# Attention: the weighted values of a row tile's eight heads in one run of 128 products instead of two runs of 64, with twelve slots of transposed exponentials

## The chip, the cores and the metric

The kernel runs on one core of a Trainium2 chip. The metric is the device time of one execution in microseconds (us), lower is better. Before the change it is 2987.2 us, the median of 3 runs (2986.61 to 2988.67).

## The reference, cut to what matters

Eight graphs (the batch) of 1024 nodes with 256 features pass through four layers, each behind a layer norm with ReLU and with a residual. The change touches the second, an attention with eight heads of 32 features, whose scores are multiplied by the adjacency matrix before the softmax:

```python
q, k, v = (proj(Wq, bq), proj(Wk, bk), proj(Wv, bv))      # 8 heads of 32
scores = jnp.einsum('bhqd,bhkd->bhqk', q, k) * SCALE
scores = scores * (adj_matrix + bond_matrix)[:, None]     # both are adj
attn = jax.nn.softmax(scores, axis=-1)
ctx = jnp.einsum('bhqk,bhkd->bhqd', attn, v)
return jnp.einsum('bse,fe->bsf', ctx.reshape(...), Wo) + bo
```

All data is float32; the matrix of adjacencies is 1024 x 1024 for each graph.

## The kernel before

The program runs the batch elements one after the other, all four layers of one before the next. The order of the work on each engine is written out by hand; engines meet through counting semaphores (`signal`), of which the name tells what is ready (`exps`: exponentials, `T_ps`: transposes in PSUM, `pv_ps`: weighted values in PSUM).

The attention part of an element is a pipeline over 64 **units**. Unit u is one head of one row tile: 128 query rows (tile t = u // 8) against all 1024 keys. For each unit:

- TensorE makes the scores, 128 x 1024, in two products (L1288), into one of two pairs of PSUM banks.
- VectorE multiplies them by the adjacency rows and takes the row maximum in one pass, `Z`, 128 x 1024 (L790). GpSimd negates the maximum (L566, `nm`).
- ScalarE takes the exponential in place with its row sum (L1046). `Z` has three slots (`ZS`).
- TensorE transposes `Z` in eight 128 x 128 blocks (L1310) into two of three PSUM banks in turn, four blocks to a bank.
- ScalarE copies the first bank out (L1036) and VectorE the second (L745) to a **slot** of transposed exponentials, `PT(u)`, 128 x 8 x 128. For the unit with u % 8 = 5, ScalarE copies both. The eight slots lie in three tiles: `PTa` four, `PTz` one, `PTb` three.
- TensorE multiplies `v` by the slots (L1339, weighted values): a product has 32 output rows, one head, and four heads stand side by side in the array. A group of four heads needs 32 products in the program, which are 64 TensorE instructions in the trace (two each). Each row tile has two groups (`GROUPS`), in two parts of PSUM bank 7.

Once both groups of a row tile are done, VectorE multiplies them by the spread inverse sums (`normalise`, L758, `ctxn`), TensorE multiplies by the output weights (`project`, L1122 on `Wo,ctxn`) and VectorE adds the result to `x` (L765).

Every engine walks the same steps u = 0, 1, ... On TensorE step u is: `project` if one is due, `scores(u + 2)`, weighted values of a group if one is due, `transposes(u)`, and the spread of the inverse sums if due. A group g is due at step 4g + 7: the first group of row tile t at step 8t + 7, the second at 8t + 11. On VectorE step u is: `Z(u)`, then `normalise`, `add_output` and statistics where they are due, then the copy of unit u - 2. On ScalarE it is the exponential of u, then the copy of unit u - 1. GpSimd also builds the 0/1 matrix `H` for the next layer in the steps' gaps (L578).

Behind the last row tile TensorE starts the third layer with `first_edges` (L1369, L1370), then the last `project` and `sum_up` (L1403). The matrix `adjT`, on whose place `PTa`, `Z` and `PTz` lie in the attention part, is loaded again in three parts by SyncE as its tenants are done (L486). At the start of the part the stacked operands `qS` and `kS` are put together by DMAs out of `khi`, `klo`, `qhi` and `qlo` (L411); `PTb` lies behind these four.

Of the kernel before, what the change touches and what calls it, by code (L numbers as in the profile page):

```python
# [5 lines left out]
F32 = mybir.dt.float32  # L6
# [25 lines left out]
def build_program(nc, x_in, adj_in, adjT_in, mask_in, wqkT0, wv0, w1attn, bq1, bk1, bv1, bo1,  # L32
# [13 lines left out]
    BOTH = 5  # L46
    PTS = 8
    PTA = 4
# [15 lines left out]
    with ctx:  # L64
# [3 lines left out]
        def signal(name, per):  # L68
            return Signal(ctx.enter_context(nc.semaphore(name)), per)
# [50 lines left out]
        def _bytes(shape):  # L120
            n = 4
            for s in shape[1:]:
# [34 lines left out]
             ("W1", [P, 3, DT, D], F32)],  # L157
            [("stacked", [P, 4, GROUPS, N], F32), ("PTb", [P, PTS - PTA - 1, NT, P], F32), ("rs", [P, HEADS, HD], F32), ("Rs", [P, GROUPS, P], F32)],
            [("h2", [P, NT, HID], F32), ("h2T", [P, FT, N], F32)],
# [6 lines left out]
        khi, klo, qhi, qlo, hT1, W1 = p1a  # L166
        _, PTb, rs, Rs = p1b
        h2, h2T = p2
# [81 lines left out]
        PT_dve = signal("PT_dve", UNITS - NT)  # L250
        pv_ps = signal("pv_ps", NT * GROUPS)
        R_ps = signal("R_ps", NT)
# [61 lines left out]
        INVERT, SPREAD, COPY, WEIGH, NORMALISE, PROJECT, ADD = 4, 4, 7, 7, 9, 10, 11  # L314
        PARTS = (NT,)

# [24 lines left out]
        def turn_bank(use):  # L341
            return 4 + turns.index(use) % TBANKS
# [56 lines left out]
        def PT(u):  # L399

            slot = u % PTS
            return PTa[:, slot] if slot < PTA else PTz if slot == PTA else PTb[:, slot - PTA - 1]

        def heads_of(t):
            return t[:, :].rearrange("p (a n) -> p a n", n=P)
# [11 lines left out]
        def _(sp):  # L417
# [38 lines left out]
            def batch(b, last):  # L456
# [30 lines left out]

                sp.wait_ge(*pv_ps(b, NT * GROUPS - 1))
                stand(sp, waited_sp)
# [130 lines left out]
        def _(dve):  # L620
# [49 lines left out]
            def batch(b, last):  # L670
# [67 lines left out]
                def evacuate(u):  # L738
                    if evacuates_both(u):
                        return  # L740
                    bank = turn_bank((u, 1))
                    dve.wait_ge(*T_ps(b, 2 * u + 2))
                    if u >= PTS:
                        dve.wait_ge(*pv_ps(b, (u - PTS) // HPG + 1))
                    dve.tensor_copy(PT(u)[:, NT // 2:NT], heads_of(ps[:, bank])).then_inc(PT_dve.sem, 1)  # L745

                def inverse_sums(t):
# [4 lines left out]
                def normalise(t):  # L752
                    dve.wait_ge(*pv_ps(b, GROUPS * (t + 1)))
                    if t == NT - 1:
                        dve.wait_ge(*Rss(b, t + 1))
                    if t:
                        dve.wait_ge(*o_ps(b, t))
                    dve.tensor_tensor(ctxn[:], ps[:, 7, 0:GROUPS * P].rearrange("p (g n) -> p g n", n=P), Rs[:],  # L758
                                      ALU.mult).then_inc(ctxs.sem, 1)
# [206 lines left out]
        def _(act):  # L966
# [8 lines left out]
            def batch(b, last):  # L975
# [52 lines left out]

                def evacuate(u):
                    for half_of_u in range(1 + evacuates_both(u)):  # L1030
                        bank = turn_bank((u, half_of_u))
                        act.wait_ge(*T_ps(b, 2 * u + half_of_u + 1))
                        if u >= PTS:
                            act.wait_ge(*pv_ps(b, (u - PTS) // HPG + 1))
                        first = NT // 2 * half_of_u
                        act.activation(PT(u)[:, first:first + NT // 2], heads_of(ps[:, bank]), ACT.Copy).then_inc(PT_act.sem, 1)  # L1036
# [81 lines left out]
        def _(pe):  # L1118
# [46 lines left out]
            def batch(b, first):  # L1165
# [155 lines left out]

                def weighted_values(g, part):


                    if part == 0:
                        pe.wait_ge(*PT_act(b, by_act(HPG * g + HPG - 1)))
                        t = g // GROUPS
                        if g == 0:
                            pe.wait_ge(*vs(b, NT // 2))
                        if g % GROUPS and t < NT - 1:  # L1330
                            pe.wait_ge(*Rss(b, t + 1))
                        if g % GROUPS == 0 and t:
                            pe.wait_ge(*ctxs(b, t))
                    for kt in range(sum(PARTS[:part]), sum(PARTS[:part + 1])):
                        if kt == NT // 2:
                            pe.wait_ge(*PT_dve(b, by_dve(HPG * g + HPG - 1)))
                        for j in range(HPG):
                            hd = ORDER[HPG * (g % GROUPS) + j]
                            mm = pe.matmul(ps[HD * j:HD * j + HD, 7, P * (g % GROUPS):P * (g % GROUPS + 1)],  # L1339
                                           v[:, kt, HD * hd:HD * hd + HD], PT(HPG * g + j)[:, kt],  # L1340
                                           start=(kt == 0), stop=(kt == NT - 1))
                    if part == len(PARTS) - 1:
                        mm.then_inc(pv_ps.sem, 1)

# [27 lines left out]
                for u in range(STEPS):  # L1372
# [6 lines left out]
                    if u + 2 < UNITS:  # L1379
                        scores(u + 2)  # L1380
                    for part in range(len(PARTS)):
                        if (g := group_due(u, WEIGH + part)) is not None:
                            weighted_values(g, part)
                    if u in BESIDE:
# [196 lines left out]
```

## Time and profile before

| | |
|---|---|
| median of 3 runs | 2987.2 us |
| span of the profiled execution, first to last instruction | 2986.1 us |
| TensorE matmul busy | 2935.2 us (98%) |
| TensorE weight load busy | 2371.0 us (79%) |
| VectorE busy | 1879.2 us (63%) |
| ScalarE busy | 1491.5 us (50%) |
| GpSimd busy | 720.8 us (24%) |
| mean granted TensorE clock | 0.999 of full speed |
| chain of work that ended last | TensorE 68%, VectorE 14%, issue 11%, GpSimd 4%, ScalarE 3% |

The profile gives for the profiled execution its span, and no device time of its own beside it; the span lies 1.1 us under the median of the timed runs. The busy shares are means over four layers with different limits, so what the change does has to be read from the attention part of one batch element. In the element used below that part runs from about 455 us to 602 us of the span. Within it a row tile of eight units repeats every 16.6 us.

### The profile page before, as it was taken

The numbers are of one execution on the slowest core, as the hardware profiler recorded it, in microseconds if no ns is written. First come the engines' busy times: TensorE is split into PE (matmuls) and PEld (weight loads), VectorE is DVE, ScalarE is ACT, GpSimd is POOL, SyncE is SP. The second block draws the span as 40 slices with busy tenths as digits, with TensorE's granted clock in tenths as the row PEclk, the third lists the DMA queues.
The fourth block names the chain that finished last, engine by engine and source line by source line (L and its number), as shares of the span: only waits on it lengthen the run. The fifth ranks groups of instructions, "written<-read, shape, count | busy, mean of one in ns | idle before, by whom it ended". The sixth has DMA issues, their size and how long they took to land.

```text
span 2986.1 us, 63496 instructions
## 1 busy us (share of the span) xinstructions
PE 2935.2 (98%) x23040; PEld 2371.0 (79%) x23040; DVE 1879.2 (63%) x4154; ACT 1491.5 (50%) x2761; POOL 720.8 (24%) x1305
## 2 busy tenths in 40 slices
PE   8999999999999999999999999999999999999999
PEld 7888787887878878888788886888868888688886
DVE  3797427874278742887428874388643886438863
ACT  2883317833288232873228732387323873238622
POOL 0343003420134201342013420134201341014410
PEclk9999999999999999999999999999999999999999
DMA  5202212022120231101311113111222022220200
GB/s 175 93 2 93 91 58 93 2 92 111 49 83 13 81 131 38 74 34 60 135 48 61 54 50 124 61 48 59 62 108 78 30 73 69 87 81 27 83 8 14
DMA packets 95317, 204.29 MB, mean 68 GB/s; under 512 B 10512, under 2 KB 41616, under 8 KB 94992
## 3 DMA queue, kind: packets, MB, share of 16 engines
q1 hardware_dynamic: 93456, 195.76, 17.9%
q8 instruction: 203, 3.33, 0.5%
q0 software_dynamic: 1536, 4.20, 0.4%
q14 instruction: 122, 1.00, 0.1%
HBM read 136.75 MB, written 8.65 MB: 49 GB/s over the span
## 4 chain that ended last, share of the span: by engine, by line
PE 68%; DVE 14%; issue 11%; POOL 4%; ACT 3%; DVEq 0%; DMA 0%; POOLq 0%; ACTq 0%; SPq 0%
PE ps L1122 39%; PE ps L1310 8%; PE ps L1403 7%; PE ps L1288 4%; PE ps L1478 4%; PE ps L1339 4%; DVE junk L832 3%; POOL H L578 3%; DVE Z L790 2%; DVE stats L629 1%; DVE h L848 1%; DVE dn L841 1%; DVE h L866 1%; POOL nm L566 1%; PE ps L1162 1%
## 5 line engine op out<-in xcount | busy, mean ns | idle before, releaser
L790 DVE CUSTOM_DVE_ANT_0 Z<-ps,adjN 128x1024 f32<-128x1024 f32 x512 | 624.0, 1219 | 69.3 <-PE ps L1288 67.1
L1046 ACT ACTIVATE Z<-Z,nm 128x1024 f32<-128x1024 f32 x512 | 587.4, 1147 | 54.2 <-POOL nm L566 54.1
L1310 PE MATMUL ps<-ident,Z 128*128 128x128 f32 x4096 | 545.9, 276 | 19.4 <-ACT Z L1046 16.9
L1310 PEld LDWEIGHTS ps<-ident,Z 128*128 128x128 f32 x4096 | 458.6, 140 | 129.4 <-issue 59.7
L1288 PE MATMUL ps<-kS,qS 128*128 128x512 f32 x1024 | 370.2, 444 | 3.3 <-issue 3.3
L578 POOL TENSOR_SCALAR H<-adjN 128x128 fp32r<-128x128 f32 (+1 forms) x456 | 316.6, 694 | 0.0
L566 POOL TENSOR_TENSOR nm<-nm,minus 128x1 f32<-128x1 f32 x512 | 97.1, 190 | 646.9 <-DVE nm L790 642.1
L1122 PE MATMUL ps<-mh,adjT 128*128 128x256 f32 x1024 | 223.6, 379 | 0.8 <-issue 0.8
L1122 PE MATMUL ps<-v,P 128*128 128x257 f32 x1024 | 223.6, 379 | 0.0
L1122 PE MATMUL ps<-hT,t3T 128*128 128x512 f32 x512 | 221.0, 592 | 0.0
L1122 PEld LDWEIGHTS ps<-v,P 128*128 128x128 f32 x1024 | 193.8, 189 | 31.9 <-issue 3.8
L1122 PEld LDWEIGHTS ps<-mh,adjT 128*128 128x128 f32 x1024 | 193.9, 190 | 27.2 <-issue 1.2
L745 DVE COPY PTa<-ps 128x512 f32<-128x512 f32 x256 | 176.0, 687 | 31.8 <-PE ps L1310 31.8
L1122 PEld LDWEIGHTS ps<-hT,t3T 128*128 128x128 f32 x512 | 97.3, 190 | 119.1 <-issue 118.6
L543 POOL TENSOR_SCALAR ve<-mv 128x4 f32<-128x4 f32 x64 | 12.6, 197 | 724.5 <-DVE mv L634 723.9
L686 DVE CUSTOM_DVE_ANT_0 E<-ps,G 128x256 f32<-128x256 f32 x64 | 27.2, 425 | 252.4 <-PE ps L1122 209.4
L1122 PE MATMUL ps<-W,hT 128*128 128x256 f32 x768 | 178.3, 382 | 0.8 <-ACT hT L980 0.8
L1036 ACT ACTIVATE PTb<-ps 128x512 f32<-128x512 f32 x256 | 144.2, 588 | 59.0 <-PE ps L1310 59.0
L1288 PEld LDWEIGHTS ps<-kS,qS 128*128 128x128 f32 x1024 | 159.5, 191 | 13.9 <-issue 8.2
L1036 ACT ACTIVATE PTa<-ps 128x512 f32<-128x512 f32 x256 | 150.8, 589 | 38.9 <-PE ps L1310 38.9
L1106 ACT ACTIVATE E<-ps,cj 128x512 f32<-128x512 f32 x128 | 87.9, 687 | 159.6 <-PE ps L1122 159.6
L1122 PEld LDWEIGHTS ps<-W,hT 128*128 128x128 f32 x768 | 143.5, 192 | 23.9 <-issue 1.0
(183 smaller groups left out, 5713.5 us busy)
## 6 DMA issues: line engine op xcount, KB each, us to landing
adjT<-adjT_in SPq DMA_DIRECT2D x8, 4096.0 KB, 13.0
adjN<-adj_in SPq DMA_DIRECT2D x8, 4096.0 KB, 17.6
adjT<-adjT_in SPq DMA_DIRECT2D x8, 2048.0 KB, 7.7
qS<-qhi SPq DMA_DIRECT2D x112, 128.0 KB, 2.1
qS<-qlo SPq DMA_DIRECT2D x112, 128.0 KB, 2.1
adjT<-adjT_in SPq DMA_DIRECT2D x8, 1536.0 KB, 12.0
xn<-x_in SPq DMA_DIRECT2D x8, 1024.0 KB, 5.7
out<-x SPq DMA_DIRECT2D x8, 1024.0 KB, 4.8
```

The source lines that it names most:

```text
L566: pool.tensor_tensor(nm[:, u:u + 1], nm[:, u:u + 1], minus[:], ALU.mult).then_inc(nms.sem, 1)
L578: done = pool.tensor_scalar(H[:, t, of], adjN[:, t, of], 0.0, 0.0, ALU.is_equal, ALU.is_equal)
L745: dve.tensor_copy(PT(u)[:, NT // 2:NT], heads_of(ps[:, bank])).then_inc(PT_dve.sem, 1)
L790: dve.tensor_tensor_reduce(Z[:, u % ZS], ps[:, 2 * (u % 2):2 * (u % 2) + 2].rearrange("p a n -> p (a n)"), adjN[:, u // HEADS], SCORE_SCAL ...
L1036: act.activation(PT(u)[:, first:first + NT // 2], heads_of(ps[:, bank]), ACT.Copy).then_inc(PT_act.sem, 1)
L1046: act.activation(Z[:, u % ZS], Z[:, u % ZS], ACT.Exp, bias=nm[:, u:u + 1], accum_out=sm[:, u:u + 1]).then_inc(exps.sem, 1)
L1122: mm = pe.matmul(dst, lhsT, rhs, start=(i == 0), stop=(i == len(pairs) - 1))
L1288: mm = pe.matmul(ps[:, 2 * (u % 2) + s], qS[:, hd, rows(t)], kS[:, hd, half(s)], start=True, stop=True)
L1310: mm = pe.transpose(ps[:, turn_bank((u, s)), rows(a)], Z[:, u % ZS, rows(NT // 2 * s + a)], ident[:])
L1339: mm = pe.matmul(ps[HD * j:HD * j + HD, 7, P * (g % GROUPS):P * (g % GROUPS + 1)], v[:, kt, HD * hd:HD * hd + HD], PT(HPG * g + j)[:, kt], ...
L1403: mm = pe.matmul(dst(n, i), lhs(n, j, i), rhs(n, j, i), start=(j == 0 and i == 0), stop=(j == NT - 1 and i == 0))
L1478: mm = pe.matmul(ps[:, bank(t), 0:D], HT[:, j, rows(t)], (Vh, Vl)[i][:, j], start=(j == 0 and i == 0), stop=(j == NT - 1 and i == 0))
```

## The change

The weighted values of both groups of a row tile are made in one run, `weighted_values(t)`, due where the second group was: step 8t + 11. The run at step 8t + 7 is gone. For that, a row tile's first four slots are held four units longer, and there are twelve slots instead of eight. The four new ones, `PTc`, lie behind `khi` and `klo`, where `qhi` and `qlo` are, so the copies of unit 8, the first into `PTc`, wait for the seven DMAs that read `qhi` and `qlo` (`qS_in`). `pv_ps` counts row tiles instead of groups, and all waits on it are rewritten. The last row tile uses slots 4 to 11 so that `PTa` is free once the last but one is done, and SyncE's first part of the `adjT` reload waits for that.

```diff
     BOTH = 5
-    PTS = 8
+    PTS = 12
     PTA = 4
...
              ("W1", [P, 3, DT, D], F32)],
-            [("stacked", [P, 4, GROUPS, N], F32), ("PTb", [P, PTS - PTA - 1, NT, P], F32), ("rs", [P, HEADS, HD], F32), ("Rs", [P, GROUPS, P], F32)],
+            [("keys", [P, 2 * GROUPS * N + 16], F32), ("PTc", [P, PTA, NT, P], F32), ("PTb", [P, PTS - 2 * PTA - 1, NT, P], F32), ("rs", [P, HEADS, HD], F32), ("Rs", [P, GROUPS, P], F32)],
             [("h2", [P, NT, HID], F32), ("h2T", [P, FT, N], F32)],
...
         PT_dve = signal("PT_dve", UNITS - NT)
-        pv_ps = signal("pv_ps", NT * GROUPS)
+        pv_ps = signal("pv_ps", NT)
         R_ps = signal("R_ps", NT)
...
         INVERT, SPREAD, COPY, WEIGH, NORMALISE, PROJECT, ADD = 4, 4, 7, 7, 9, 10, 11
-        PARTS = (NT,)
...
-            slot = u % PTS
+            slot = u % PTS if u < UNITS - HPG else u % PTS + HPG
+            if slot >= 2 * PTA:
+                return PTc[:, slot - 2 * PTA]
             return PTa[:, slot] if slot < PTA else PTz if slot == PTA else PTb[:, slot - PTA - 1]
...
-                sp.wait_ge(*pv_ps(b, NT * GROUPS - 1))
+                sp.wait_ge(*pv_ps(b, NT - 1))
                 stand(sp, waited_sp)
...
                     bank = turn_bank((u, 1))
+                    stacks_read(u)
                     dve.wait_ge(*T_ps(b, 2 * u + 2))
                     if u >= PTS:
-                        dve.wait_ge(*pv_ps(b, (u - PTS) // HPG + 1))
+                        dve.wait_ge(*pv_ps(b, (u - PTS) // HEADS + 1))
                     dve.tensor_copy(PT(u)[:, NT // 2:NT], heads_of(ps[:, bank])).then_inc(PT_dve.sem, 1)
+
+                def stacks_read(u):
+                    if u == 2 * PTA:
+                        for s in range(NH):
+                            for j in range(len(qS_in[s])):
+                                dve.wait_ge(*qS_in[s][j](b, 64))
...
                 def normalise(t):
-                    dve.wait_ge(*pv_ps(b, GROUPS * (t + 1)))
+                    dve.wait_ge(*pv_ps(b, t + 1))
                     if t == NT - 1:
...
                 def evacuate(u):
+                    if u == 2 * PTA:
+                        for s in range(NH):
+                            for j in range(len(qS_in[s])):
+                                act.wait_ge(*qS_in[s][j](b, 64))
                     for half_of_u in range(1 + evacuates_both(u)):
...
                         if u >= PTS:
-                            act.wait_ge(*pv_ps(b, (u - PTS) // HPG + 1))
+                            act.wait_ge(*pv_ps(b, (u - PTS) // HEADS + 1))
                         first = NT // 2 * half_of_u
...
-                def weighted_values(g, part):
-
-
-                    if part == 0:
-                        pe.wait_ge(*PT_act(b, by_act(HPG * g + HPG - 1)))
-                        t = g // GROUPS
-                        if g == 0:
-                            pe.wait_ge(*vs(b, NT // 2))
-                        if g % GROUPS and t < NT - 1:
-                            pe.wait_ge(*Rss(b, t + 1))
-                        if g % GROUPS == 0 and t:
-                            pe.wait_ge(*ctxs(b, t))
-                    for kt in range(sum(PARTS[:part]), sum(PARTS[:part + 1])):
-                        if kt == NT // 2:
-                            pe.wait_ge(*PT_dve(b, by_dve(HPG * g + HPG - 1)))
-                        for j in range(HPG):
-                            hd = ORDER[HPG * (g % GROUPS) + j]
-                            mm = pe.matmul(ps[HD * j:HD * j + HD, 7, P * (g % GROUPS):P * (g % GROUPS + 1)],
-                                           v[:, kt, HD * hd:HD * hd + HD], PT(HPG * g + j)[:, kt],
-                                           start=(kt == 0), stop=(kt == NT - 1))
-                    if part == len(PARTS) - 1:
-                        mm.then_inc(pv_ps.sem, 1)
+                def weighted_values(t):
+
+                    if t == 0:
+                        pe.wait_ge(*vs(b, NT // 2))
+                    else:
+                        pe.wait_ge(*ctxs(b, t))
+                    if t < NT - 1:
+                        pe.wait_ge(*Rss(b, t + 1))
+                    for g in range(GROUPS):
+                        first = HEADS * t + HPG * g
+                        pe.wait_ge(*PT_act(b, by_act(first + HPG - 1)))
+                        for kt in range(NT):
+                            if kt == NT // 2:
+                                pe.wait_ge(*PT_dve(b, by_dve(first + HPG - 1)))
+                            for j in range(HPG):
+                                hd = ORDER[HPG * g + j]
+                                mm = pe.matmul(ps[HD * j:HD * j + HD, 7, P * g:P * (g + 1)],
+                                               v[:, kt, HD * hd:HD * hd + HD], PT(first + j)[:, kt],
+                                               start=(kt == 0), stop=(kt == NT - 1))
+                    mm.then_inc(pv_ps.sem, 1)
...
                         scores(u + 2)
-                    for part in range(len(PARTS)):
-                        if (g := group_due(u, WEIGH + part)) is not None:
-                            weighted_values(g, part)
+                    if (t := tile_due(u, WEIGH)) is not None:
+                        weighted_values(t)
                     if u in BESIDE:
```

The order of TensorE's instructions shows the move. In the listings the names are those of tiles: `Z` on `ident` are transposes, `kS,qS` are scores, `rs` is the spread of the inverse sums, `PTa`, `PTz`, `PTb` and `PTc` on `v` are weighted values; a listing gives program instructions, of which a float32 product becomes two in the trace where its source does. The first place is TensorE from step 14 to step 17 of the first batch element, at the transposes of unit 14. Before:

```order
L1310 MATMUL ps<-ident,Z 128x128 x8
L1288 MATMUL ps<-kS,qS 128x512 x2
L1339 MATMUL ps<-PTa,v 32x128 x32
L1310 MATMUL ps<-ident,Z 128x128 x8
L1288 MATMUL ps<-kS,qS 128x512 x2
L1310 MATMUL ps<-ident,Z 128x128 x8
L1318 MATMUL ps<-ident,rs 128x128 x2
L1288 MATMUL ps<-kS,qS 128x512 x2
L1310 MATMUL ps<-ident,Z 128x128 x8
```

Now:

```order
L1322 MATMUL ps<-ident,Z 128x128 x8
L1300 MATMUL ps<-kS,qS 128x512 x2
L1322 MATMUL ps<-ident,Z 128x128 x8
L1300 MATMUL ps<-kS,qS 128x512 x2
L1322 MATMUL ps<-ident,Z 128x128 x8
L1330 MATMUL ps<-ident,rs 128x128 x2
L1300 MATMUL ps<-kS,qS 128x512 x2
```

The run of 32 products on `PTa` between the scores of unit 17 and the transposes of unit 15 is gone; nothing else moved.

The second place is TensorE at steps 18 and 19, beginning with the scores of unit 20. Before (the last two rows come seven more times):

```order
L1288 MATMUL ps<-kS,qS 128x512 x2
L1310 MATMUL ps<-ident,Z 128x128 x8
L1288 MATMUL ps<-kS,qS 128x512 x2
L1339 MATMUL ps<-PTz,v 32x128
L1339 MATMUL ps<-PTb,v 32x128 x3
```

Now:

```order
L1300 MATMUL ps<-kS,qS 128x512 x2
L1322 MATMUL ps<-ident,Z 128x128 x8
L1300 MATMUL ps<-kS,qS 128x512 x2
L1350 MATMUL ps<-PTc,v 32x128 x32
L1350 MATMUL ps<-PTa,v 32x128 x32
L1322 MATMUL ps<-ident,Z 128x128 x8
```

Where 32 products on slots 4 to 7 stood, 64 stand now: first those of the row tile's first four heads (`PTc`), then those of the other four (`PTa`), and the transposes of unit 19 come behind both.

## Rows read from the trace of the kernel before

**Rows 1.** The page of the profile: its first line, and one line of DMA issues.
```profile
span 2986.1 us, 63496 instructions
...
qS<-qlo SPq DMA_DIRECT2D x112, 128.0 KB, 2.1
```

**Rows 2.** Windows view, one row tile: start:end, then busy us and (instructions) of each engine.
```profile
503.30:519.90 16.60, 16.36 (x219) 13.68 (x221) 15.02 (x29) 14.19 (x27) 7.20 (x17) 1.00 0.01 2
```

**Rows 3.** Chain of work that ended last, second batch element: start, us, what.
```profile
486.74 1.88 PE ps L1339 x64
...
569.72 1.88 PE ps L1339 x64
```

**Rows 4.** Timeline, all engines, 511 to 529: start, us, engine, instruction, [idle before <-releaser].
```profile
513.67 1.09 PE L1310 MATMUL ps<-ident,Z 128*128 128x128 f32 x8
...
514.80 0.69 DVE L745 COPY PTb<-ps 128x512 f32<-128x512 f32 x1 [0.63 <-PE ps L1310]
...
515.46 1.23 DVE L790 CUSTOM_DVE_ANT_0 Z<-ps,adjN 128x1024 f32<-128x1024 f32 x1
...
516.08 0.71 PE L1288 MATMUL ps<-kS,qS 128*128 128x512 f32 x2
...
516.62 1.04 PE L1310 MATMUL ps<-ident,Z 128*128 128x128 f32 x8
...
517.00 1.15 ACT L1046 ACTIVATE Z<-Z,nm 128x1024 f32<-128x1024 f32 x1 [0.42 <-POOL nm L566]
...
518.37 1.09 PE L1310 MATMUL ps<-ident,Z 128*128 128x128 f32 x8 [0.24 <-ACT Z L1046]
...
519.21 0.72 PE L1288 MATMUL ps<-kS,qS 128*128 128x512 f32 x2
...
519.86 0.31 PE L1339 MATMUL ps<-PTb,v 128*32 128x128 f32 x3
...
521.53 0.28 PE L1339 MATMUL ps<-PTb,v 128*32 128x128 f32 x3
...
521.74 1.09 PE L1310 MATMUL ps<-ident,Z 128*128 128x128 f32 x8
...
521.88 0.42 DVE L758 TENSOR_TENSOR ctxn<-ps,Rs 128x256 f32<-128x256 f32 x1
...
522.87 0.69 DVE L745 COPY PTa<-ps 128x512 f32<-128x512 f32 x1 [0.57 <-PE ps L1310]
...
527.16 1.15 ACT L1046 ACTIVATE Z<-Z,nm 128x1024 f32<-128x1024 f32 x1
527.30 1.22 DVE L790 CUSTOM_DVE_ANT_0 Z<-ps,adjN 128x1024 f32<-128x1024 f32 x1 [0.29 <-PE ps L1288]
```

**Rows 5.** Waits, 486.74 to 586.3 (six row tiles): who waited: us, times, longest.
```profile
DVE PTb L745 <- PE ps L1310: 3.8, 6, 0.6
DVE PTa L745 <- PE ps L1310: 3.4, 6, 0.6
```

**Rows 6.** Timeline, all engines, 476 to 485 (start of the attention part).
```profile
477.85 1.16 ACT L1046 ACTIVATE Z<-Z,nm 128x1024 f32<-128x1024 f32 x1
...
479.60 0.60 SPq L411 DMA_DIRECT2D qS<-qlo  x1
...
481.62 0.69 DVE L745 COPY PTb<-ps 128x512 f32<-128x512 f32 x1 [0.57 <-PE ps L1310]
```

**Rows 7.** Timeline, all engines, 593 to 602 (end of the attention part).
```profile
593.90 1.14 ACT L1046 ACTIVATE Z<-Z,nm 128x1024 f32<-128x1024 f32 x1
...
596.54 1.09 PE L1310 MATMUL ps<-ident,Z 128*128 128x128 f32 x8
...
597.88 0.30 PE L1339 MATMUL ps<-PTz,v 128*32 128x128 f32 x1
...
599.76 0.39 PE L1369 MATMUL ps<-hh,H 128*128 128x258 f32 x1
...
600.96 1.13 PE L1122 MATMUL ps<-Wo,ctxn 128*128 128x256 f32 x4 [0.22 <-DVE ctxn L758]
```

More of the change, by code:

```diff
@@ L166, in build_program @@
         khi, klo, qhi, qlo, hT1, W1 = p1a
-        _, PTb, rs, Rs = p1b
+        _, PTc, PTb, rs, Rs = p1b
         h2, h2T = p2
```

## The prediction

> **What bounds the kernel now.** I read the windows first, then the chain, then the timeline of one row tile, then the waits, then the two ends of the attention part.
>
> The windows view of one row tile [rows 2] shows TensorE busy for 16.36 of 16.60 us, VectorE 15.02, ScalarE 14.19 and GpSimd 7.20, with the granted clock at 1.00. That looks like a kernel bound by TensorE with VectorE 9% behind, but such shares don't tell who waits for whom. The chain of work that ended last gives the pace: second runs of weighted values start at 486.74 and 569.72 with four between, so a row tile takes (569.72 - 486.74) / 5 = 16.60 us [rows 3]. The profile's page gives the span of 2986.1 [rows 1], against which the sum below is made; the median of the timed runs is 1.1 us above it.
>
> The timeline of row tile 2 and 3 [rows 4] shows how the two engines pass the limit between them. Three places matter.
>
> At the second run (step 27): scores start at 519.21, the run at 519.86, and the transposes of unit 27 behind it at 521.74. VectorE does `Z(29)` meanwhile, so it gets through almost the whole run; `ctxn` starts at 521.88, as soon as the run is done. Then it waits 0.57 us for the transposes (copy at 522.87). From here TensorE sets the pace until VectorE's `Z(32)` at 527.30, which waited 0.29 for its scores.
>
> At the first run (the one of the row tile before ends where the transposes of unit 23 start, 513.67): VectorE waits 0.63 us for them (copy at 514.80).
>
> After that VectorE sets the pace: its copy leads to `Z(26)` at 515.46, over GpSimd's negation to the exponential at 517.00 (waited 0.42 for GpSimd), which ends a little before TensorE's transposes of unit 26 at 518.37 (waited 0.24 for ScalarE). So TensorE has a little idle time ahead of the second run, and VectorE none. The waits view over six row tiles [rows 5] has both waits once in each: 3.8 and 3.4 us in 6 times each. This is all that VectorE loses to the two runs: 1.2 us in a row tile, though they hold TensorE for 3.8 us, because a run of 1.9 us is nearly covered by the VectorE work that is queued up when it starts.
>
> **The change, part by part.**
>
> The length of a run. From scores to the next transposes TensorE takes 521.74 - 519.21 = 2.53 us with a run between and 516.62 - 516.08 = 0.54 without [rows 4], so a run costs it 1.99. The last of its sixteen packs of four instructions starts 1.67 after the first of the rows, 519.86 and 521.53, so a pack takes 0.11 and sixteen more take 1.76. The other 0.23 is paid at the run's two ends. The long run therefore costs 1.99 + 1.76 = 3.75, and a row tile's total on TensorE falls by 0.23.
>
> The added part, 64 instructions more at step 8t + 11: +1.76 us. The work that covers the run now, `Z(29)`, ends just when the present run does (`ctxn` starts at 521.88, 0.07 behind the run's end). `Z(30)` stands behind `ctxn` and the copy of unit 27 on VectorE, and both wait for the run; ScalarE's exponential of unit 29 stands behind the copy of unit 27 too. So nothing is left to cover the added 1.76, and all that follows on all three engines moves by it: `ctxn`, transposes of unit 27, `Z(32)` from 527.30 to 529.06. Bounds: 1.76 if nothing covers it; 1.53 if the 0.23 of the saved ends fell here, which I exclude, since those ends are at the other run.
>
> The removed part, the run ahead of the transposes of unit 31 (as of unit 23 in the rows). Those transposes start one row tile after 513.67, at 530.27 now. Without the run they start when the exponential of unit 31 is done. It starts at 527.16 + 1.76 = 528.92, takes 1.24 to its end and the next 0.12 to the transposes (517.00 to 518.37 is 1.37 in all): 530.29. So on TensorE the delay is fully made up at this point, and this is the trap: VectorE isn't made up. It is 1.76 late at `Z(32)`, works without a pause until the copy of unit 31, and there it finds its transposes done, so the 0.63 wait is gone. Behind that copy it is late by 1.76 - 0.63 = **1.13 us**, and from there VectorE sets the pace up to the transposes of unit 34 and the next run. Each row tile is 1.13 longer, 17.73 instead of 16.60. Bounds: had `Z(32)` also won back its 0.29 wait, 0.84; but that wait is for scores that moved with the rest. If only half of the 0.63 comes back, because TensorE or ScalarE is late behind the exponential of unit 31, 1.45. I take 1.13.
>
> There are six such distances from run to run in one element (row tile 0 to 6).
>
> The start. Row tile 0 loses its first run. Copy of unit 7 waited 0.57 there (481.62), the exponential of unit 7 starts at 477.85 and so its transposes could start at 479.2 [rows 6]: **-0.57**. From zero to that.
>
> The end. Behind row tile 6's run the exponential of unit 63 moves by 1.76, from 593.90 to 595.66, and its transposes can start 1.37 later, at 597.03, where they stood at 596.54 [rows 7]. The last run starts 597.88 - 596.54 = 1.34 behind them, at 598.37, and takes 599.76 - 597.88 + 1.76 = 3.64: `first_edges` at 602.01 instead of 599.76. The last `project` stood 1.20 behind `first_edges`, 0.22 of it waiting for `ctxn`, a wait that is gone since `ctxn` needs only the run: 602.01 + 0.98 = 602.99 instead of 600.96, **+2.0**. Up to +2.6 if the spread of the sums ahead of the run is late with the exponential. The next layer starts from there with TensorE without a gap, so I see nothing that gives it back.
>
> The new slots. `PTc` makes both copies of unit 8 wait for the last `qS` DMA. It is issued at 479.60 and lands 2.1 later [rows 6, 1], at 481.7; the first copy of unit 8 comes more than half a microsecond behind the start of the copy of unit 7, now at 481.05, so at about 482. Cost nothing; if the landing took 3 us, 0.6 an element. The wait instructions themselves run while the exponential and `Z` ahead of them do. All other waits on `pv_ps` ask for a run at least one step old, so cost nothing. The earlier reload of `adjT` gives nothing: no engine is in the chain for it.
>
> The sum for one element: -0.57 + 6 x 1.13 + 2.0 = 8.2 us; for eight, 65.7. 2986.1 + 65.7 = 3051.8 as a span, and with the 1.1 of the median above it **3053 us**, 2.2% slower.
>
> **The rivals.**
>
> *TensorE's work alone counts (faster).* TensorE is busy for 16.36 of 16.60 us; if it were the bound throughout, the place of the runs would not matter and each row tile would gain the 0.23 of one run's two ends: 64 x 0.23 = 15, so 2972. This decides once VectorE's and ScalarE's queued work at the run's start is longer than the run, 3.75; it is 521.88 - 519.86 = 2.0 in the rows. Against it speak both waits of rows 5 as well. 6%. The Trainium skill has the rule behind this rival (TensorEngine Tiling (Array Packing), Key Properties): changing the tiling mode of the array drains it. Half the runs are half the changes between 128 x 128 and 128 x 32. The trace agrees that the ends cost something, the 0.23 above; by the rule alone the change would be the gain of 15 us, by the trace it is the smaller term.
>
> *The delay is made up (no change, or little).* TensorE is back on time at unit 31, 530.29 against 530.27. If VectorE could follow, each row tile would cost nothing and the ends remain: 8 x (2.0 - 0.57) = 11, so 2998; with the start's gain alone and the end covered, 2983. VectorE has no slack in between, so 6% for both, of which 3% within 0.2%.
>
> *Half made up, or less than in the forecast.* A row tile costs 0.3 to 0.8: 3010 to 3035. 8%.
>
> *Nothing is won back.* 1.76 a row tile, 2.6 at the end, nothing at the start: 8 x (10.6 + 2.6) = 106, so 3093; with half of the wait won back, 3068 to 3075. 6% beyond the range.
>
> **How the numbers follow.** The forecast, with the bounds of its terms from 1.0 to 1.4 a row tile, has 74% and spans 3040 to 3072. The range is 3030 to 3072; about 2 in 10 is left out. A measurement of this kernel can't tell less than about 0.2% (6 us) from no change. Faster by more than that: 7%. Within it: 4%. Slower: 89%.
>
> **What the changed kernel's profile would show.** Runs of 128 instructions 17.7 us apart, each about 3.6 us long. VectorE's wait ahead of `ctxn` new, 1.6 to 1.8 us each; the 0.57 behind it as now; the 0.63 at the copies of units with u % 8 = 7 gone. VectorE busy for the same time in a longer row tile, and TensorE at 16.1 of 17.7. The exponential of units with u % 8 = 2 still waits for GpSimd. The prediction is wrong if `ctxn` waits under 1 us (then more work covers the run than I see), if a wait for `qS` DMAs stands ahead of the copies of unit 8, or if the row tile takes 16.4.

## The result and the profile after

The changed kernel takes 3039.97 us, the median of 4 runs (3038.86 to 3041.77), against 2987.93 for the kernel before beside it. The ratio is 1.0176, with a 95% interval of 1.0162 to 1.019: 52 us slower, where 3053 (66 us slower) was forecast, in a range of 3030 to 3072. The profiled execution has a span of 3037.1, 51.0 more than before. The page's first lines:

```profile
span 3037.1 us, 63580 instructions
...
PE 2956.9 (97%) x23040; PEld 2362.0 (78%) x23040; DVE 1873.8 (62%) x4154; ACT 1490.7 (49%) x2761; POOL 721.0 (24%) x1305
```

TensorE has the same 23040 instructions and is busy 22 us longer by the page: the busy time of pipelined matmuls is no count of work.

The chain of work that ended last (start, us, what) gives the pace as in [rows 3]: second batch element, the first and the sixth run of weighted values, the last one, and the start of the third layer's sums.

```profile
492.79 3.63 PE ps L1350 x128
...
580.44 3.63 PE ps L1350 x128
...
610.03 3.63 PE ps L1350 x128
...
615.43 11.22 PE ps L1412 x94
```

A row tile takes (580.44 - 492.79) / 5 = 17.53 us instead of 16.60. It is so in all eight batch elements: by the starts of `ctxn` on VectorE, row tile 1 to 5, a row tile takes 17.46 to 17.58, where it took 16.57 to 16.60. The timeline of one row tile (all engines, 526 to 546), in the order of [rows 4]:

```profile
527.13 0.72 PE L1300 MATMUL ps<-kS,qS 128*128 128x512 f32 x2
...
527.77 0.30 PE L1350 MATMUL ps<-PTz,v 128*32 128x128 f32 x1
...
531.40 1.09 PE L1322 MATMUL ps<-ident,Z 128*128 128x128 f32 x8
531.54 0.42 DVE L766 TENSOR_TENSOR ctxn<-ps,Rs 128x256 f32<-128x256 f32 x1 [1.71 <-PE ps L1350]
...
532.53 0.69 DVE L747 COPY PTa<-ps 128x512 f32<-128x512 f32 x1 [0.57 <-PE ps L1322]
...
536.96 1.23 DVE L798 CUSTOM_DVE_ANT_0 Z<-ps,adjN 128x1024 f32<-128x1024 f32 x1 [0.29 <-PE ps L1300]
...
538.12 1.15 PE L1322 MATMUL ps<-ident,Z 128*128 128x128 f32 x8
...
540.25 0.18 DVE L635 BATCH_NORM_AGGREGATE mv<-stats 128x2 f32<-128x6 f32 x1
540.34 0.66 DVE L747 COPY PTb<-ps 128x512 f32<-128x512 f32 x1
...
540.92 1.22 DVE L798 CUSTOM_DVE_ANT_0 Z<-ps,adjN 128x1024 f32<-128x1024 f32 x1
```

The run lies between the scores at 527.13 and the transposes at 531.40: 4.27 us, 3.73 more than the 0.54 without a run. `ctxn` (L766) has a wait of 1.71 ahead of it that was not there before; the wait of 0.57 at the copy behind it, and that of 0.29 at `Z(32)` (536.96), are as they were. The copy of unit 31 (540.34), where 0.63 was waited, starts without a wait. The waits view over six row tiles (492.79 to 598) shows the new wait as the only one of its size on VectorE:

```profile
DVE ctxn L766 <- PE ps L1350: 10.3, 6, 1.7
```

At the start of the attention part (timeline of the changed kernel, 476 to 492) the copy of unit 7 (487.72) no longer waits. The last `qS` DMA is issued at 487.04, lands 2.1 later by the page's median [rows 1], at about 489.14, and the first copy into `PTc`, of unit 8, starts at 489.30. The exponential's last piece, its row sum, starts 0.13 ahead of that copy, where it is 0.09 at the copy of unit 7, so the new DMA waits cost 0.04 at most here. The margin of 0.16 is thin, though.

```profile
483.60 1.22 DVE L798 CUSTOM_DVE_ANT_0 Z<-ps,adjN 128x1024 f32<-128x1024 f32 x1 [1.90 <-PE ps L1300]
...
487.04 0.60 SPq L412 DMA_DIRECT2D qS<-qlo  x1
...
487.72 0.69 DVE L747 COPY PTb<-ps 128x512 f32<-128x512 f32 x1
...
489.30 0.60 ACT L1048 ACTIVATE PTc<-ps 128x512 f32<-128x512 f32 x1
```

To measure the two ends, two lines of the kernel before are needed beside [rows 3]: its `Z(8)` in the timeline, and its start of the third layer's sums in the chain.

```profile
476.85 1.22 DVE L790 CUSTOM_DVE_ANT_0 Z<-ps,adjN 128x1024 f32<-128x1024 f32 x1 [1.89 <-PE ps L1288]
```

```profile
602.09 11.22 PE ps L1403 x94
```

From `Z(8)` to the first full run: 486.74 - 476.85 = 9.89 before, 492.79 - 483.60 = 9.19 after, so -0.70. From there to the third layer's sums: 602.09 - 486.74 = 115.35 before, 615.43 - 492.79 = 122.64 after, +7.29, of which six row tiles take 6 x 0.93 = 5.6 and the end 1.7. Per element 6.6, for eight 53; the spans differ by 51.0.

### The profile page after: what moved, and what is told of

Same layout as the page of the kernel before. It is cut to its first block, busy times and chain, and to the rows that moved or that the text cites. A ratio compares the mean times of both kernels' runs of the same rounds, so it can differ in the third digit from the quotient of the medians.

```text
span 3037.1 us, 63580 instructions
## 1 busy us (share of the span) xinstructions
PE 2956.9 (97%) x23040; PEld 2362.0 (78%) x23040; DVE 1873.8 (62%) x4154; ACT 1490.7 (49%) x2761; POOL 721.0 (24%) x1305
## 4 chain that ended last, share of the span: by engine, by line
PE 67%; DVE 14%; issue 9%; ACT 3%; POOL 3%; SPq 2%; DMA 1%; DVEq 0%; POOLq 0%; ACTq 0%
PE ps L1134 37%; PE ps L1322 7%; PE ps L1350 7%; PE ps L1412 7%; PE ps L1487 4%; PE ps L1300 4%; DVE junk L840 3%; POOL H L579 2%; DVE Z L798 2%; SPq L412 2%; DVE stats L630 1%; ACT Z L1058 1%; DVE h L856 1%; DVE dn L849 1%; DVE h L874 1%
## 5 line engine op out<-in xcount | busy, mean ns | idle before, releaser
L1322 PEld LDWEIGHTS ps<-ident,Z 128*128 128x128 f32 x4096 | 448.6, 140 | 216.3 <-issue 126.9
L1322 PE MATMUL ps<-ident,Z 128*128 128x128 f32 x4096 | 557.2, 279 | 52.4 <-ACT Z L1058 40.9
L927 DVE TENSOR_TENSOR P<-E,adjT 128x512 f32<-128x512 f32 x128 | 88.7, 693 | 113.6 <-ACT E L1118 113.6
L553 POOL TENSOR_SCALAR ve<-mv 128x2 f32<-128x2 f32 x32 | 6.1, 191 | 575.8 <-DVE mv L635 575.8
L1048 ACT ACTIVATE PTc<-ps 128x512 f32<-128x512 f32 x176 | 101.8, 587 | 60.8 <-PE ps L1322 58.7
```

Of the source, the lines that this page charges most:

```text
L1322: mm = pe.transpose(ps[:, turn_bank((u, s)), rows(a)], Z[:, u % ZS, rows(NT // 2 * s + a)], ident[:])
```

## The experiments

Theory 1 is that of the prediction: a run of weighted values is paid for by how much longer it holds TensorE than the work that VectorE and ScalarE have in hand when it starts (its cover), about 2.0 us. Against it stand: the slots and waits that the change brings; a price for each run, or for being one run, whatever its length; and TensorE's own work as the bound. Each time below is a median, with its ratio to the kernel before on the same chip.

**Two runs again, with twelve slots.** The changed kernel with one edit:

```diff
-                def weighted_values(t):
+                def weighted_values(t, g):
...
-                    for g in range(GROUPS):
+                    if True:
...
-                    mm.then_inc(pv_ps.sem, 1)
+                    if g == GROUPS - 1:
+                        mm.then_inc(pv_ps.sem, 1)
...
-                    if (t := tile_due(u, WEIGH)) is not None:
-                        weighted_values(t)
+                    if (n := group_due(u, WEIGH)) is not None:
+                        weighted_values(n // GROUPS, n % GROUPS)
```

> The changed kernel with its twelve slots, its waits and its reload, but with the weighted values again in two runs of 64, at steps 8t + 7 and 8t + 11. Theory 1 (the length of the run beyond what VectorE has in hand costs the time): back to 2988, within 6 us, a row tile in 16.6. Rival (slots in other places, copies of unit 8 that wait, later waits on pv_ps): half of the 52 us or more stays, 3014 or above.

Measured: 2984.62, ratio 0.999 (0.998 to 0.9999). Its chain has the row tile back at (570.66 - 487.67) / 5 = 16.60:

```profile
487.67 1.88 PE ps L1351 x64
...
570.66 1.89 PE ps L1351 x64
```

The three waits ahead of the products are shared out between the two runs as they were before. So all 52 us belong to the runs. Slots, their places, the DMA waits, the later waits on `pv_ps` and the earlier reload of `adjT` cost nothing that can be measured.

**One run, shorter.** The changed kernel with fewer key blocks in its one run; a quarter of the weighted values' products is left out (96 of the 128 instructions of a run remain), and in a second kernel half (64). For 96:

```diff
-                        for kt in range(NT):
-                            if kt == NT // 2:
-                                pe.wait_ge(*PT_dve(b, by_dve(first + HPG - 1)))
+                        pe.wait_ge(*PT_dve(b, by_dve(first + HPG - 1)))
+                        for kt in range(6):
...
```

> The changed kernel with the weighted values over the first six of eight key blocks only (a quarter of the products is left out), still in one run. Theory 1 says that beyond the cover each us of the run is a us of the row tile: 0.88 less in each of six distances and at the end, a row tile in 16.65, 7 x 0.88 x 8 = 49 off 3040: 2991, and VectorE's wait ahead of ctxn 0.83. Rival (one run costs by being one, whatever its length): 3020 or above.

> The changed kernel with the weighted values over the first four of eight key blocks only (half of the products is left out), still in one run. Theory 1: another 0.88 a row tile less, to 15.8, since the wait ahead of ctxn just reaches zero: 2941. If the cover were longer than 2.0 us the slope from 96 to 64 would be below the one from 128 to 96. Rival as for 96 products: 3010 or above.

Measured: 2984.48 with 96 (0.9993, 0.9984 to 1.0003) and 2930.24 with 64 (0.9811, 0.9795 to 0.9827). The chains of the two kernels, and the wait of `ctxn` with 96 products over the six to seven row tiles from 486 to 590:

```profile
486.72 2.76 PE ps L1349 x96
...
570.02 2.76 PE ps L1349 x96
```

```profile
DVE ctxn L766 <- PE ps L1349: 5.9, 7, 0.8
```

```profile
480.00 1.88 PE ps L1349 x64
...
558.92 1.88 PE ps L1349 x64
```

A row tile takes 17.53, 16.66 and 15.78 us with 128, 96 and 64 instructions: 0.87 and 0.88 less for each 32, which is what 32 instructions take (eight packs of 0.11). The slope is one all the way from 128 to 64, and the wait ahead of `ctxn` falls from 1.71 over 0.8 to nothing. That is what theory 1 says. A price for being one run is out: with one run of 64 the row tile is 0.82 below the 16.60 with two, and the prediction's removed part alone, measured below, is 0.80. That 0.82 is also what the first of two runs of 64 costs, of the 1.99 for which it holds TensorE: such a run is covered in part, not free, and no kernel here has one run shorter than 64. Both times lie under what was expected, 2991 and 2941. The expectation counts seven places where a run is shorter, six distances and the end, but row tile 0 has a run too: 8 x 0.88 x 8 = 56, against 55.5 and 54.2 measured for each step. One more thing stands in these numbers: one run of 96, a quarter of the work gone, takes as long as the kernel before with all of it.

**Four runs of 32.** The kernel before with `PARTS = (NT // 2, NT // 2)`, which its code allows.

> The kernel before with four runs of 32 in a row tile, at steps 8t + 7, 8, 11 and 12. Theory 1: each run now takes 1.1 us and is covered, so VectorE's waits of 0.63 and 0.57 mostly go, but TensorE pays two more pairs of ends, 0.46 a row tile on top of 16.36, and becomes the bound: row tile 16.6 to 16.8, 2988 to 3003. If run ends cost TensorE nothing: row tile 16.1 to 16.4, 2950 to 2975. If short runs are not covered either: 2988 with the waits still there.

Measured: 3034.67, ratio 1.0159 (1.0143 to 1.0176). This missed all three expectations. The timeline around one of the runs, scores and the transposes behind it, and the chain:

```profile
512.07 0.71 PE L1288 MATMUL ps<-kS,qS 128*128 128x512 f32 x2
...
513.73 1.09 PE L1310 MATMUL ps<-ident,Z 128*128 128x128 f32 x8
```

```profile
512.79 1.01 PE ps L1339 x32
...
582.52 1.01 PE ps L1339 x32
```

The run costs 1.66 - 0.54 = 1.12, as expected, so the ends of a run cost 0.25 here too, and two more pairs are 0.5. But the row tile takes (582.52 - 512.79) / 4 = 17.43, 0.83 more. The waits view (450 to 610) shows what the expectation had missed:

```profile
DVE ctxn L758 <- PE ps L1339: 9.4, 7, 1.3
...
PE ps L1122 <- DVE PTz L745: 3.8, 7, 0.6
```

`ctxn` waits 1.3 us in each row tile, and TensorE 0.55 for VectorE ahead of the projection. The last of the four runs stands at step 8t + 12, behind the scores of unit 8t + 14 and the transposes of unit 8t + 11, while `ctxn` stays at step 8t + 13 on VectorE, ahead of copies whose transposes are done. The expectation has no such wait. So this kernel tested a late `ctxn` together with short runs.

**Four runs, each a step earlier.** The same with all four runs and the copy of the spread sums a step earlier, so that the last run is where the second run of 64 was (`-` is the kernel before):

```diff
-        INVERT, SPREAD, COPY, WEIGH, NORMALISE, PROJECT, ADD = 4, 4, 7, 7, 9, 10, 11
-        PARTS = (NT,)
+        INVERT, SPREAD, COPY, WEIGH, NORMALISE, PROJECT, ADD = 4, 4, 6, 6, 9, 10, 11
+        PARTS = (NT // 2, NT // 2)
```

> The kernel before with four runs of 32 in a row tile, each one step earlier than in the last trial of four runs: steps 8t + 6, 7, 10 and 11, so that the last one is where the second run of 64 was, a step ahead of the scores of unit 8t + 14 and not behind them (the copy of the spread sums on ScalarE is a step earlier too). If the 47 us that four runs cost came from ctxn waiting 1.3 us for a run that stood behind those scores, and from TensorE waiting 0.65 for VectorE ahead of the projection, both waits go and only the ends remain, 2 x 0.24 a row tile less the 0.24 that TensorE waits now: a row tile in 16.8 to 16.9, 2997 to 3005. If the number of runs alone costs it: 3025 to 3040.

> The same kernel as the four runs a step earlier, timed again in more rounds, since 2984 against 2988 is near what a measurement can tell: 2981 to 2985, ratio 0.998 to 0.9995, if the 0.8 us an element that its trace gained at the end of the attention part are real.

Measured: 2984.35 (0.9987, 0.9977 to 0.9997), and in the second timing of the same kernel 2985.15 (0.9989, 0.998 to 0.9998). `ctxn` of the second and the sixth row tile, and the two waits that the kernel before has in [rows 5] (window 486 to 585):

```profile
503.54 0.42 DVE L758 TENSOR_TENSOR ctxn<-ps,Rs 128x256 f32<-128x256 f32 x1
...
570.00 0.42 DVE L758 TENSOR_TENSOR ctxn<-ps,Rs 128x256 f32<-128x256 f32 x1
```

```profile
DVE PTb L745 <- PE ps L1310: 3.1, 6, 0.5
...
DVE PTa L745 <- PE ps L1310: 1.7, 6, 0.3
```

Both large waits are gone, which confirms the reading of the trial before: its 47 us came from the place of the last run against `ctxn`. The row tile takes (570.00 - 503.54) / 4 = 16.62, not the expected 16.8 to 16.9. VectorE's waits behind the runs are 0.5 and 0.3 instead of 0.6 and 0.6, and still the row tile is no shorter, though the runs are half as long: of the 0.4 that VectorE gains there, 0.3 goes in gaps that the view doesn't list, 0.19 at the copy at 560.29 and 0.12 at the one at 568.20. So cutting both runs in two gains nothing in the row tile. The 0.1% by which the kernel is faster lies at the ends of the attention part. The last two `ctxn` of the element are 11.59 apart (586.97 and 598.56) instead of 11.88 (588.62 and 600.50 in the kernel before), and about as much in each of the eight elements, 0.3 of the 0.8 us that the expectation of the second timing names; the rest lies ahead of an element's first `ctxn` and was not taken apart. That second timing, 2985.15, is 0.15 above its expected range, its ratio inside. This kernel is the fastest of all kernels here that do the whole computation, together with the two runs on twelve slots, from which it can't be told.

**The run ahead of the scores.** The kernel before with the two calls of a step exchanged; no instruction more or less:

```diff
-                    if u + 2 < UNITS:
-                        scores(u + 2)
                     for part in range(len(PARTS)):
                         if (g := group_due(u, WEIGH + part)) is not None:
                             weighted_values(g, part)
+                    if u + 2 < UNITS:
+                        scores(u + 2)
```

> The kernel before with its two runs of 64, each ahead of the scores of its step and not behind them. Instructions and lengths are the same. Theory 1: VectorE has one Z less, 1.2 us, in hand when a run starts, so it waits for scores as well: 0.8 more at the second run and 0.6 at the first, 1.4 a row tile, 3050 to 3090. Rival (what a run costs depends on its length and ends alone): 2988.

Measured: 3056.26, ratio 1.0228 (1.0211 to 1.0245). The waits (486 to 585), and `ctxn` of two row tiles five apart:

```profile
DVE Z L790 <- PE ps L1288: 15.9, 16, 1.5
```

```profile
497.03 0.42 DVE L758 TENSOR_TENSOR ctxn<-ps,Rs 128x256 f32<-128x256 f32 x1
...
586.44 0.42 DVE L758 TENSOR_TENSOR ctxn<-ps,Rs 128x256 f32<-128x256 f32 x1
```

`Z` waits for scores 16 times in this stretch, up to 1.5 us each: 1.45 at the second run (ahead of the `Z` at 513.76) and 1.23 at the first (505.19), where copies waited 0.57 and 0.63 in the kernel before. The waits of copies are gone, and the 0.29 of once a row tile is as before. The row tile takes (586.44 - 497.03) / 5 = 17.88, 1.28 more (expected: 1.4). Runs of the same length and number cost 68 us more when VectorE has one `Z` less in hand. With the kernels of 96 and 64 products this is the other half of theory 1: length against cover.

**The statistics in the wait.** The changed kernel with VectorE's statistics of a row tile moved into the wait ahead of the next `ctxn`:

```diff
                     if (t := tile_due(u, NORMALISE)) is not None:
+                        if t:
+                            dve.wait_ge(*x1s(b, t))
+                            statistics(b, 2, t - 1, x[:, t - 1])
+                            aggregate(b, 2, t - 1)
                         normalise(t)
...
-                    if (t := tile_due(u, ADD + 1)) is not None:
+                    if (t := tile_due(u, ADD + 1)) == NT - 1:
...
```

> The changed kernel with VectorE's statistics of a finished row tile (L630 and L635) moved from steps 8t + 16 and 17 into the wait ahead of ctxn in the next row tile. Theory 1 (VectorE sets the pace from the scores of a row tile's first unit to the next run): the moved 0.45 us leave each row tile, 17.1 instead of 17.5, about 25 off 3040: 3015. Rival (TensorE or ScalarE sets the pace there): 3040, unchanged.

Measured: 3026.69, ratio 1.0132 (1.0115 to 1.0149), 13 us less than the changed kernel. `ctxn` of two row tiles five apart:

```profile
510.60 0.42 DVE L766 TENSOR_TENSOR ctxn<-ps,Rs 128x256 f32<-128x256 f32 x1 [1.04 <-PE ps L1354]
...
596.79 0.42 DVE L766 TENSOR_TENSOR ctxn<-ps,Rs 128x256 f32<-128x256 f32 x1 [1.04 <-PE ps L1354]
```

A row tile takes (596.79 - 510.60) / 5 = 17.24, 0.29 less. So VectorE does set the pace between `Z(32)` and the next run, as said, and TensorE doesn't. That only two thirds of the expected 0.45 come back is no second limit. The stretch where the statistics stood, from `Z(32)` to `Z(34)`, took 540.92 - 536.96 = 3.96 in the changed kernel; in this one it takes 536.92 - 533.26 = 3.66, with no wait in either:

```profile
533.26 1.23 DVE L798 CUSTOM_DVE_ANT_0 Z<-ps,adjN 128x1024 f32<-128x1024 f32 x1 [0.29 <-PE ps L1304]
...
536.92 1.22 DVE L798 CUSTOM_DVE_ANT_0 Z<-ps,adjN 128x1024 f32<-128x1024 f32 x1
```

The statistics held 0.30 of VectorE's order there, not 0.45, and all of it comes back.

**The projection three steps later.** The kernel before with `project` and `add_output` at steps 8t + 17 and 18, and the statistics behind them three steps later too; the last row tile stays as it was.

```diff
+        def tile_late(u, lag):
+            t = tile_due(u, lag)
+            if t == NT - 1:
+                return t
+            t = tile_due(u - 3, lag)
+            return t if t != NT - 1 else None
...
-                    if (t := tile_due(u, PROJECT)) is not None:
+                    if (t := tile_late(u, PROJECT)) is not None:
...
```

> The kernel before with the output projection of a row tile and its addition three steps later, at step 8t + 17, where TensorE waited 0.24 for ScalarE, instead of 8t + 14, between the two runs. If the runs and the projection standing close together make VectorE wait: up to 0.3 a row tile less, 2972 to 2980. If VectorE's and TensorE's work is only moved: 2988. If the projection then delays the transposes of unit 18 and what hangs on them: up to 3000.

Measured: 3018.02, ratio 1.0101 (1.0084 to 1.0118), worse than every expectation. Its timeline (510 to 530) around the projection:

```profile
517.26 0.20 DVE L758 RECIPROCAL sm<-sm 128x8 f32<-128x8 f32 x1 [0.79 <-ACT Z L1054]
...
519.77 0.69 DVE L753 COPY PTb<-ps 128x512 f32<-128x512 f32 x1 [0.50 <-PE ps L1318]
...
522.19 0.42 DVE L773 TENSOR_TENSOR x<-ps,x 128x256 f32<-128x256 f32 x1 [0.54 <-PE ps L1130]
...
523.27 0.66 PE L1318 MATMUL ps<-ident,Z 128*128 128x128 f32 x4 [0.22 <-DVE PTa L753]
```

The addition now stands ahead of a copy on VectorE and waits 0.54 for the projection, and the transposes wait 0.22 for the bank that this copy was to free. The largest wait is another: with addition and statistics gone from in front of it, the reciprocal of the row sums reaches its turn early and waits 0.79 for ScalarE. In all VectorE waits 0.79 + 0.50 + 0.54 = 1.83 in a row tile, where it was 0.63 + 0.57 + 0.29 = 1.49. The projection's place between the two runs was the better one.

**Two runs a step earlier.** The kernel before with everything from the spread sums on one step earlier (`... = 4, 4, 6, 6, 8, 9, 10`).

> The kernel before with its two runs of 64 and all that follows from them (spread sums on ScalarE, ctxn, projection, addition) one step earlier, steps 8t + 6 and 8t + 10. A shift as a whole keeps the distances, so a row tile stays at 16.6 and only the end of each element can gain, where the transposes of unit 63 no longer stand behind a run but only those of unit 62: 0 to 1 us an element, 2980 to 2988. If instead the shift brings a run and a copy of unit 8t + 5 (both halves on ScalarE) together, up to 3000.

Measured: 2993.06, ratio 1.0014 (1.0005 to 1.0023), slightly slower. The two copies that wait for a run in its timeline:

```profile
507.17 0.69 DVE L745 COPY PTa<-ps 128x512 f32<-128x512 f32 x1 [0.57 <-PE ps L1310]
...
516.03 0.69 DVE L745 COPY PTb<-ps 128x512 f32<-128x512 f32 x1 [1.20 <-PE ps L1310]
```

The wait behind the second run is 0.57 as before, that behind the first is 1.20 instead of 0.63. The shift didn't keep all distances, and the row tile is not the expected 16.6: by the starts of `ctxn` at 506.18 and 573.89 it takes 16.93. The first run now stands a step ahead, right behind the unit whose both halves ScalarE copies, so VectorE has no copy in hand when it starts. The run and the last instruction that VectorE has in hand, in this kernel and in the one before:

```profile
513.01 1.95 PE L1339 MATMUL ps<-PTa,v 128*32 128x128 f32 x64
...
514.63 0.20 DVE L750 RECIPROCAL sm<-sm 128x8 f32<-128x8 f32 x1
```

```profile
511.79 1.95 PE L1339 MATMUL ps<-PTa,v 128*32 128x128 f32 x64
...
513.99 0.17 DVE L634 BATCH_NORM_AGGREGATE mv<-stats 128x2 f32<-128x6 f32 x1
```

VectorE is done 1.82 behind the run's start instead of 2.37, 0.55 less, and waits 0.57 more: a run of the same length with less cover, as theory 1 has it. The rows also show why a run of 1.9 us isn't free behind a cover of over 2: the copy needs the transposes behind the run as well, and starts 1.13 behind their start in both kernels (514.90, not shown, to 516.03; 513.67 to 514.80 in [rows 4]). Run and transposes less the cover give the wait, 1.89 + 1.13 - 1.82 = 1.20 here and 1.88 + 1.13 - 2.37 = 0.64 before. The row tile is 0.33 longer; that over six row tiles in eight elements is 16 us, of which the total shows 4; the rest comes back outside of these six distances and was not taken apart.

## Why the prediction was right

The direction, the mechanism and the range held, and the places are those that it named. The size came out at an edge: 3040 is the lower end of the inner span of 3040 to 3072, and a row tile's 0.93 lies just under the 1.0 to 1.4 on which that span was built. By its own steps:

- **The length of a run.** Forecast 3.75 for the long one; measured 3.73 (527.13 to 531.40, less 0.54). The 0.23 at its ends are about 0.25 with runs of 32 and 64 and 128 instructions alike (1.12, 1.99 and 3.73, less 0.109 a pack).
- **The added part**, forecast 1.76 from the run to `Z(32)`: from the first row of the run to that `Z` it was 527.30 - 519.86 = 7.44 before [rows 4] and is 536.96 - 527.77 = 9.19, 1.75 more. Nothing covers it, and the kernels with 96 and 64 products show that each us of the run is one of the row tile down to a run as long as before.
- **The removed part.** This is the term that was mis-sized. Forecast was that VectorE gets back the 0.63 it waited at the copy of unit 31. From `Z(32)` to `Z(34)` it took 515.46 + 16.60 - 527.30 = 4.76 before [rows 4]; it takes 540.92 - 536.96 = 3.96, 0.80 less. The listed wait is only the time in which VectorE did nothing at all. Without it the copy starts 0.09 behind the start of the aggregation ahead of it (540.25 and 540.34), whose 0.18 it now overlaps, and the next `Z` starts 0.58 behind the copy's start instead of 0.66. So a row tile is longer by 1.75 - 0.80 = 0.95, measured 0.93, forecast 1.13. This alone is 6 x 0.2 x 8 = 10 of the 13 us that the forecast was too high.
- **TensorE is back on time at unit 31, VectorE is not.** Shown: the transposes of unit 31 start 538.12 - 527.77 = 10.35 behind the run's start, where the forecast has 530.29 - 519.86 = 10.43. The row tile is longer all the same, and the kernel with the moved statistics shows that it is VectorE's work from there that counts.
- **The start**, forecast -0.57, measured -0.70, the same effect once more.
- **The end**, forecast +2.0, measured +1.7.
- **The new slots and waits**, forecast nothing: shown by the two runs on twelve slots.
- **TensorE's share.** Forecast 16.1 us busy of 17.7. By the windows view it is 16.80 of 17.54 (527.84 to 545.38), more than the 16.36 of before, though the engine has the same instructions and fewer ends. The sum does not use this figure.

The rival by which TensorE's work alone counts gave 2972 and falls with the result; the kernel with the run ahead of the scores has the same TensorE work as the one before and is 68 us slower. The rule behind it in the Trainium skill (TensorEngine Tiling (Array Packing), Key Properties) is that a change of the tiling mode drains the array. The trace agrees as far as it goes: a run costs about 0.25 us apart from its length. That the drain is what takes them, no run here separates. For 64 runs fewer it makes 16 us of TensorE time, which nobody waited for.

The kernel with four runs a step earlier, whose ends cost TensorE 0.5 us more a row tile and which is no slower, says how little they weigh.

What stays open is what the kernels with four runs a step earlier and with two runs a step earlier gain at the start of the attention part, and what a single run shorter than 64 would cost.

## What to carry to other kernels

Before joining short bursts on a shared engine into a long one, read how much work each consumer has in hand when the burst starts, here 2.0 us. Past that each us counts in full: VectorE waited 0.6 behind each of two bursts of 1.9 us, and 2.3 for one of 3.6. Up to it a burst is covered in part and not free, since a consumer also waits for the work that stands behind the burst, here 1.1 us of transposes: one burst of 1.9 us cost 0.8, and four of 1.0 us gave no shorter row tile than two of 1.9. What the engine saves by switching less counts only if it is waited for. And when a burst is moved, look at the first instruction in each consumer's order that needs it: a `ctxn` that needed a later run cost nearly as much as the change itself, and exchanging two calls cost more.

## What the runs showed of the hardware

A wait in the profile can be worth more than its listed idle time: removing one of 0.63 us on VectorE gave 0.80 back. Without the wait the copy starts 0.09 behind the start of an instruction of 0.18, which it overlaps, and the next instruction 0.58 behind the copy instead of 0.66. In the same way work taken out can be worth less than it is listed with: the moved statistics are listed with 0.42 + 0.18 = 0.60 us and gave 0.30 back.

The cost of going from full products to products of 32 columns and back is about the same 0.25 us on TensorE for runs of 32, 64 and 128 instructions, and within a run four instructions take 0.11 us.
